# First layer: the decay's two low-rank products by halves of the tokens

## What is computed

```
xw = h + xx * mu_w                      # (B, T, 256)
w = w0 + jnp.tanh(xw @ wA) @ wB         # wA is 256 x 64, wB is 64 x 256
decay = jnp.exp(-jnp.exp(w))
S = decay[..., None] * S + k v          # one step for each token
```

## Time and profile before

| | us |
|---|---|
| median of three runs | 4898.1 |
| the profiled execution | 4895.12 |
| its span, first to last instruction | 4893.3 |
| mean granted TensorE clock | 0.953 |
| TensorE busy | 4312.8 (88%) |
| VectorE busy | 3747.4 (77%) |
| GpSimd busy | 3038.0 (62%) |
| ScalarE busy | 2534.9 (52%) |

### The profile page before, as it was taken

The page is one execution under the profiler, slowest core; times in us unless marked ns, Lnnn a source line. Parts: engine busy times, 40 slices in busy tenths (PEclk is TensorE's granted clock), DMA queues, the critical chain, the costliest instruction groups (busy, mean ns, idle before and its releaser), DMA issues. The chain is left out here.

```text
span 4893.3 us, 58342 instructions
## 1 busy us (share of the span) xinstructions
PE 4312.8 (88%) x18862; PEld 2819.8 (58%) x18862; DVE 3747.4 (77%) x5980; ACT 2534.9 (52%) x4881; POOL 3038.0 (62%) x1970
## 2 busy tenths in 40 slices
PE   5689999999999999998989899888988988499993
PEld 1345555555556555565655555555555555378883
DVE  6887778778778877775059988888988898545676
ACT  1244334434433433433468777777777777145552
POOL 3455555556555555553157888888888888555552
PEclk7899999999999999999999999999999999599997
DMA  4233332333333233332112211111222111496787
GB/s 145 80 106 108 105 99 92 110 99 113 103 109 96 95 110 97 106 110 98 39 64 81 74 69 71 67 70 69 91 78 74 69 67 67 156 246 208 254 285 279
DMA packets 302510, 545.46 MB, mean 111 GB/s; under 512 B 30593, under 2 KB 146561, under 8 KB 293249
## 3 DMA queue, kind: packets, MB, share of 16 engines
q1 hardware_dynamic: 274560, 466.08, 29.7%
q0 software_dynamic: 27648, 75.67, 4.3%
HBM read 422.71 MB, written 118.92 MB: 111 GB/s over the span
## 5 line engine op out<-in xcount | busy, mean ns | idle before, releaser
L1444 POOL TENSOR_TENSOR c_dbx<-c_dtx,c_Brep 128x1024 f32<-128x1024 f32 x512 | 1201.6, 2363 | 198.9 <-DVE c_hs L1462 100.5
L876 POOL TENSOR_TENSOR a_kv<-a_rk,a_kv 128x512 f32<-128x512 f32 x512 | 805.3, 1584 | 409.4 <-DMA a_kv<-v_rows 409.0
L1462 DVE TENSOR_TENSOR_SCAN c_hs<-psum,c_carry,c_dbx 128x512 f32<-128x512 f32 x768 | 937.3, 1266 | 122.1 <-ACT psum L1451 72.0
L885 DVE TENSOR_TENSOR_SCAN a_S<-a_decay,a_carry,a_kv 128x513 f32<-128x513 f32 x512 | 795.8, 1554 | 185.9 <-POOL a_kv L876 93.9
L1451 ACT ACTIVATE psum<-c_dt,c_cols 128x512 f32<-128x512 f32 x1024 | 697.1, 688 | 368.2 <-DVE c_hs L1462 363.4
L802 POOL TENSOR_TENSOR a_hid_e<-a_hid_e,a_g_rep 128x512 f32<-128x512 f32 x256 | 389.0, 1521 | 767.1 <-ACT a_hid_e L791 562.9
L1478 PEld LDWEIGHTS psum<-ident,c_hs 128*128 128x128 f32 x4096 | 491.6, 145 | 393.5 <-DVE c_hs L1462 216.0
L1478 PE MATMUL psum<-ident,c_hs 128*128 128x128 f32 x4096 | 616.2, 284 | 108.3 <-DVE c_hs L1462 105.0
L891 DVE TENSOR_TENSOR a_prod<-a_rk,a_S 128x512 f32<-128x512 f32 x512 | 546.9, 1068 | 70.9 <-PE psum L907 70.8
L783 PE MATMUL psum<-a_W_down,a_hid_e 128*128 128x256 f32 x2304 | 549.5, 384 | 53.9 <-POOL a_hid_e L802 29.7
L207 PE MATMUL psum<-a_xT,a_W_up 128*128 128x512 f32 x1152 | 560.7, 617 | 14.7 <-ACT a_hid_e L791 14.6
(11 more groups left out here) (266 smaller groups left out, 6829.4 us busy)
## 6 DMA issues: line engine op xcount, KB each, us to landing
a_kv<-v_rows SPq DMA_DIRECT2D x512, 256.0 KB
a_g_rep<-g_rows SPq DMA_DIRECT2D x256, 256.0 KB, 3.9
c_Brep<-b_rows SPq DMA_DIRECT2D x64, 1024.0 KB, 4.7
d_xs<-sorted_rows SPq DMA_DIRECT2D x320, 128.5 KB
d_w<-results SPq DMA_DIRECT2D x64, 512.0 KB, 11.4
d_w<-in_d_experts SPq DMA_DIRECT2D x32, 768.0 KB, 9.4
sorted_rows<-d_zeros SPq DMA_DIRECT2D x66, 128.5 KB, 6.8
a_xa<-in_L_attn_x SPq DMA_DIRECT2D x16, 512.0 KB, 4.6
```

Source lines behind the costliest of these rows:

```text
L876: m_kv[g] = pool.mark(nc.gpsimd.tensor_tensor(kv[:, g % NV, 1:C + 1], rk[slot][:, 1, hb, :], kv[:, g % NV, 1:C + 1], ALU.mult))
L885: m_scan[q] = dve.mark(nc.vector.tensor_tensor_scan(S[:, q % NS, :], decay[cq % 2][:, hb, :], kv[:, q % NV, :], carry[:, sq_:sq_ + 1], ALU ...
L1444: m_dbx[g] = m_dbx[g + 1] = pool.mark(nc.gpsimd.tensor_tensor(dbx[:, r:r + 2, :], dtx[slot][:, e, :].unsqueeze(1).broadcast_to([P, 2, C]), ...
L1462: m_scan[q] = dve.mark(nc.vector.tensor_tensor_scan(hs[:, q % NR, :], psum[:, DA + q % ND, :], dbx[:, q % NX, :], first, ALU.mult, ALU.add))
```

## The change

The product with `wA` is made for the two halves of the tokens apart: the first half goes to output partitions 0 to 63, the second to 64 to 127, both in columns 0 to 255 of the bank. `lora` becomes 128 x 512, of which 256 columns are used: the first half of the tokens on the upper partitions, the second on the lower. The tanh is one instruction of 128 x 256. `wB` is loaded twice, onto partitions 0 to 63 and 64 to 127, so that the product of each half finds its weights on its own partitions. Both banks are claimed first; the bank now stands for a half of the tokens, and holds both output blocks side by side. Four matmuls of 64 x 128 weights on 256 columns follow, the halves in turn. Of the exponentials that read PSUM there are four of 128 x 256; each waits for the last of the four matmuls, and a bank counts as free after the one for the second output block. The exp(-exp) in place stays 128 x 512. What is counted in `Columns.sent` falls from 2048 to 1024 for `wA` and from 2048 to 1024 for `wB`.

```diff
--- before.py
+++ after.py
@@ -225,7 +225,7 @@
         s_xb, s_store = ([sem(f"{n}{i}") for i in range(2)] for n in ("xb", "store"))
         W = {n: brief(n, [P, KB, D]) for n in ("Wr", "Wk", "Wv", "Wg")}
         W["Wo"] = sb("Wo", [P, KB, D])
-        wA, wB = brief("wA", [P, KB, LORA]), brief("wB", [LORA, D])
+        wA, wB = brief("wA", [P, KB, LORA]), brief("wB", [2 * LORA, D])
         w1, w2 = sb("w1", [P, KB, F]), sb("w2", [P, FB, D])
         W_up, W_down = sb("W_up", [P, SH + E, KB, P]), sb("W_down", [P, SH + E, D])
         W_router = sb("W_router", [P, KB, E])
@@ -259,7 +259,8 @@
         xT = [sb(f"xT{i}", [P, KB, C]) for i in range(2)]
         NHE, NHF, NG = 4, 2, 3
         hid_e, hid_f = sb("hid_e", [P, NHE, C]), sb("hid_f", [P, NHF, C])
-        lora = sb("lora", [LORA, C])
+        CH = C // 2
+        lora = sb("lora", [2 * LORA, C])
         gates, gT = sb("gates", [P, TL, E]), lora[0:E, :]
         g_rows = nc.dram_tensor("g_rows", (2, E, C), F32).ap()
         g_rep, s_grep = sb("g_rep", [P, NG, C]), [sem(f"grep{i}") for i in range(NG)]
@@ -277,7 +278,7 @@
 
         nc.sync.dma_start(xa[:, :, :], chunks_in[:, 0, :, :]).then_inc(s_xa, 16)
         loaded_first = load(nc, s_load, [(ident[:, :], I["ident"]), (col_pack[:, :, :], I["a_cols"]), (chunk_mask[:, :], I["chunk_mask"])])
-        loaded_mid = load(nc, s_mid, [(wA[:, :, :], I["a_wA"]), (wB[:, :], I["L0_attn_wB"])] + [(W[n][:, :, :], I["a_" + n]) for n in ("Wk", "Wr", "Wv", "Wg")] +
+        loaded_mid = load(nc, s_mid, [(wA[:, :, :], I["a_wA"]), (wB[0:LORA, :], I["L0_attn_wB"]), (wB[LORA:, :], I["L0_attn_wB"])] + [(W[n][:, :, :], I["a_" + n]) for n in ("Wk", "Wr", "Wv", "Wg")] +
                           [(of_head[:, :], I["of_head"]), (to_value[:, :, :], I["to_value"]), (same_head[:, :], I["same_head"])])
         loaded_late = load(nc, s_late, [(W["Wo"][:, :, :], I["a_Wo"]), (w1[:, :, :], I["a_w1"]), (w2[:, :, :], I["a_w2"]),
                                         (W_up[:, :, :, :], I["b_up"]), (W_down[:, :, :], I["b_down"]), (W_router[:, :, :], I["b_router"])])
@@ -456,23 +457,34 @@
                 dve.engine.wait_ge(s_mid, loaded_mid)
                 m_done["centre"] = dve.mark(nc.vector.tensor_tensor(centre[:, :], ident[:, :], same_head[:, :], ALU.subtract))
             pe.after(m)
-            m = xm_free[0] = pe.mark(matmuls(nc, bank[0:LORA, :], [(wA[:, kb, :], buf[:, kb, :]) for kb in range(KB)]))
+            for kb in range(KB):
+                for half in range(2):
+                    m = nc.tensor.matmul(bank[half * LORA:(half + 1) * LORA, 0:CH], wA[:, kb, :], buf[:, kb, half * CH:(half + 1) * CH],
+                                         start=(kb == 0), stop=(kb == KB - 1), skip_group_check=True)
+                Columns.sent += 2 * CH
+            m = xm_free[0] = pe.mark(m)
             yield
             act.after(m)
             if m_done.get("stored gates", 0):
                 act.engine.wait_ge(s_gout, 16 * m_done["stored gates"])
-            m_lora = G.freed[i] = act.mark(nc.scalar.activation(lora[:, :], bank[0:LORA, :], ACT.Tanh))
+            m_lora = G.freed[i] = act.mark(nc.scalar.activation(lora[:, 0:CH], bank[:, 0:CH], ACT.Tanh))
             yield
             products = []
             for ob in range(KB):
                 i, bank = yield from G.claim(pe)
-                pe.after(m_lora)
-                m = m_done["lora free"] = pe.mark(matmuls(nc, bank, [(wB[:, ob * P:(ob + 1) * P], lora[:, :])]))
-                products.append((i, bank, m))
-            yield
-            for ob, (i, bank, m) in enumerate(products):
-                act.after(m, *scanned)
-                m = G.freed[i] = act.mark(nc.scalar.activation(decay[slot][:, ob, 1:C + 1], bank, ACT.Exp, bias=cols["w0"][:, ob:ob + 1]))
+                products.append((i, bank))
+            pe.after(m_lora)
+            for ob, half in ((0, 0), (0, 1), (1, 0), (1, 1)):
+                m = nc.tensor.matmul(products[half][1][:, ob * CH:(ob + 1) * CH], wB[half * LORA:(half + 1) * LORA, ob * P:(ob + 1) * P],
+                                     lora[half * LORA:(half + 1) * LORA, 0:CH], start=True, stop=True, skip_group_check=True)
+            Columns.sent += 2 * C
+            m = m_done["lora free"] = pe.mark(m)
+            yield
+            act.after(m, *scanned)
+            for ob in range(KB):
+                for half, (i, bank) in enumerate(products):
+                    m = G.freed[i] = act.mark(nc.scalar.activation(decay[slot][:, ob, 1 + half * CH:1 + (half + 1) * CH], bank[:, ob * CH:(ob + 1) * CH], ACT.Exp,
+                                                                   bias=cols["w0"][:, ob:ob + 1]))
                 act.after(m)
                 m_decay = act.mark(nc.scalar.activation(decay[slot][:, ob, 1:C + 1], decay[slot][:, ob, 1:C + 1], ACT.Exp, scale=-1.0))
             in_small.clear()
```

## The result

The change made the kernel slower: 4985.4 us (median of 6 runs, 4983.35 to 4987.88) against 4901.6 for six runs of the kernel before, ratio 1.0168 with an interval of 1.0158 to 1.0178. The forecast was 4877, and the range ended at 4912. The profiled execution has a span of 4983.8 us.

A forecast was written before the change was run, and what follows sets the result against it. TensorE was taken to bound a chunk. Per chunk +0.1 (decay) - 2.1 (boundary) + 0.4 (clock) = -1.6 us, over 13 chunks -21: from 4895.1 to 4874, plus 3.0 for the median, 4877; range 4850 to 4912.

The forecast's parts named there:

- Edits 1 and 2, pairs abreast: At the wA and wB products: column halves and row halves run in pairs, each saving 0.86 us a chunk.
- What stands in the way: At the decay: waits for ScalarE's copy and third exponential eat the 1.72 us saved; net 0 to +0.1 a chunk.
- The clock: Behind the decay's wait: half a chance of a half clock costing 1.7 us; net +0.4 us a chunk.
- What moves, (a) and (b): At the chunk boundary: smaller counts put background work one unit ahead, gaining 2.1 us a chunk.
- (a): At the chunk boundary: router's chain and expert output at L815 emitted one step earlier, at step 0 instead of 1.
- (b): At the chunk boundary: gate transposes (L733) stand ahead of the first expert-down on TensorE instead of behind it.
- the wait and the clock: Rival: half clock behind the decay's wait in every chunk, no boundary gain; +1.8 a chunk, 4921 us; chance 0.18.

The follow-up runs named there:

- e9: Changed kernel, new counts, exponentials in bank order, last up product's gelu emitted before the feed-forward block, 2048 columns counted at first Wg product: 4863.8 us, ratio 0.9937.
- e1: Changed kernel with the decay counted in Columns.sent as before (2048 and 2048): 4906.5 us, ratio 1.0030.
- e2: Kernel before, instructions untouched, with the decay counted as 1024 and 1024 columns: 4934.8 us, ratio 1.0091.
- e3: Changed kernel, new counts, with both exponentials of one token half first, then the other's, then exp(-exp): 4969.3 us, ratio 1.0162.
- e4: Changed kernel with the old counts and both exponentials of one token half first, then the other's: 4889.9 us, ratio 0.9996.

## Why the prediction was wrong

- **Edits 1 and 2, pairs abreast**: right. 0.85 each against 0.86. The 0.43 us a record can't be read from the earlier trace rows alone, but in the trace the last three of its records of `a_W_up` start 0.43 apart. For the row halves, which no row showed then, 1.06 against 1.91 us decides; the Trainium skill ("TensorE: Matmul & The Clock Gate", Part 3) said so of row groups too, and the trace agrees, with a factor of 1.8 for two, the mode change in it.
- **What stands in the way**: right. Exponential 467 ns (470), wait 2.20 (2.3) behind and 1.18 (1.1) ahead; the weight loads' wait grew to 32.0 / 13 = 2.5 us, not to 3. The warning of the Trainium skill ("TensorEngine Tiling (Array Packing)", PSUM Bottleneck) held: at this place the evacuation took what tiling gave, until e9 found TensorE another bank.
- **The clock**: mis-sized. I gave half a chance to 1.7 us at one place, net +0.4. In the kernel after it falls behind all three waits; a chunk has 8.9 us more at half speed, up to 4.45. I priced the wait at the decay and gave the boundary none, where I had left a wait of some 2 us for L815 and the run has one of 3.8. But e1, e2, e3 and e4 show waits of one length with the clock falling or not, so the rows that I had could not have given the price.
- **What moves, (a) and (b)**: the step that failed. (b) was right: the gate transposes come first and the wait at the third expert-down is gone. (a) was half right: the gates are ready in step 1 instead of step 2, but the expert output at L815 stays at step 1. The planner sends the last expert-down in step 29 with the old counts and with the new: a lead of one unit only takes the last but one out of that step, and the experts are closed in step 30 in both. So the third expert-down no longer waits for GpSimd, but the first waits longer for L815. The gain of 2.1 was 0.6, less the clock's fall behind it. The bound of 0 was too narrow: an earlier gate moves VectorE's order, and the work between gate and expert output then stands in front of what TensorE waits for.
- **What I left out**: `Wg`. I followed the lead of one unit to the boundary and not through the steps between. Ahead of the second `Wg` product it puts two up products where there was one, so that this product takes the bank of the first, and TensorE gets there before VectorE has read it: 2.3 us. The wait of a transposition adds 0.84, and a table load comes at the gate. By e2 the new order costs +3.3 us a chunk where I had -2.1: 5.4 of the 8.4 us by which the chunk was off.
- **Rivals**: "the wait and the clock" had the sign and one of three places; its price (+1.8 a chunk) is near what e1 measured with the old order, +1.7, but in part by luck: there the clock falls behind `wB` in 7 chunks of 13, not in all, and falls more often at the boundary too. It took the new order to be free.

## What to carry to other kernels

Where an order is made by a meter of work sent, a cheaper operation moves all that comes after it. Run the new instructions with the old counts, and the old instructions with the new counts, before judging either: here the counts alone cost 0.9%, the instructions alone 0.3%, and both together 1.7%. And a shorter product is worth something only if what follows needs no result or bank from its readers; give it independent work first, and shorten it then.

## What was not expected of the hardware

- Two row groups of 64 and two column groups of 64 run abreast in fp32 at nearly twice the speed: 1.06 and 1.01 us for eight records of 256 columns, against 1.91 and 1.86 for four of 512.
- The length of a wait doesn't say whether the granted clock falls behind it. Behind 1.01 + 1.01 us it falls in 10 chunks of 13 in e3 and in none in e4, with the same instructions round it; behind the 2.2 us at `wB` in 13 of 13 in the kernel after and in 7 of 13 in e1; behind 2.17 to 2.53 us at `Wg` in 13 of 13 in the kernel after and in none in e2. At the boundary, waits of 2.0 to 2.7 us left it at 1.00 in 22 of 26 cases in the kernel before (one is in the earlier trace rows); the longer ones of 3.6 to 3.9 us in the kernel after never did. What else decides isn't shown here.
- Less work can mean more time at the lower clock. e3 has 1.7 us a chunk less for TensorE than e2 and 1.0 more of waits, yet 9.6 us more at half speed, and a chunk is 3.2 us longer.
